# A gated delta-rule recurrence: spreading the decays with TensorE and adding the kept state in PSUM

## The chip, the cores and the metric

The kernel runs on one core of a Trainium2 chip. The metric is the time of one execution on the device, in microseconds (us). The kernel before takes 7533.77 us, the median of 3 runs (7531.89 to 7543.39).

## The reference

Two layers over x of shape (16, 512, 256). Only the recurrent attention of the first layer matters here. It has 16 heads with keys, queries and values of 64, made from the normed x by a projection, a causal convolution over 4 tokens and a silu; a (the decay, one per head and value row) and beta are sigmoids of projections.

```python
def step(S, inp):
    qt, kt, vt, at, bt = inp
    err = jnp.einsum('bhij,bhj->bhi', S, kt) - vt
    S = at[..., None] * S - bt[..., None, None] * (err[..., None] * kt[:, :, None, :])
    o = jnp.einsum('bhij,bhj->bhi', S, qt)
    return (S, o)
```

The rest (norm and gate of o, output projection, a small expert layer, then a second layer of attention) runs after the recurrence and is not touched.

## The kernel before, in words

`layer0_recurrence` cuts the 512 tokens into chunks of C = 16 and the 16 batch entries into two groups of 8, which gives 64 steps; step s works on group s mod 2. Inside a chunk the recurrence is solved token by token on 128 partitions (8 batch entries x 16 heads); between chunks the state `st[g]` (128 partitions = two heads x 64 key rows, 8 batch entries, 8 head pairs, 64 value columns) is multiplied by the decay of the whole chunk and gets the chunk's outer products added.

Each engine has a list of its own, written out by hand: a function `slot(s, ...)` per engine, called once per step, the middle ones in a hardware loop of two slots per turn. Slot s works on several steps at once: the projections and the convolution of step s + 1, the norm, gates and first projections of step s + 2, the solve of step s, and the state update of step s - 1. The engines meet only in semaphores. Each engine, and each DMA queue (SP's and ACT's), runs its list strictly in order, so that the order of the list is part of the schedule.

- **PE** (L499 to L516): `project` of step s + 1, banks 2 to 5 (L480; banks 2 and 3 wait for the end of the solve of step s - 1, `eb` at L809, as they overwrite `rows_bank`); `update` banks 0 and 1; `gates` of step s + 2 (L461: two transposes, then two gate banks of four matmul instructions of L471 and two of L472 each); `update` banks 2 to 7; `betas`; `front2` (L435, keys and values transposed); `products` (L443); `project` banks 0 and 1 of step s + 2. `update` (L418) makes 8 banks of 8 small matmuls into two PSUM banks `d_bank` in turn. An f32 matmul stands in the trace as two MATMUL instructions.
- **ACT** (L654): copies of the convolution banks (`evict`, L529), `silu`, `seed_rows`, `place_keys`, `gates` (L631), the shares of tokens 0, 1 and 2 (`shares`, L591, which POOL needs), `betas`, `front2` (L567, which ends with the write of `v_dram`, L580), `products` (L607), `evict` of banks 0 and 1, the last shares.
- **DVE** (L812): the 18 tap groups of the convolution (`conv`, L698, L709) with the norm between them, then `decay` (L713, L717: one 128x4096 multiply of the whole state by `db`, both in SBUF), the 8 adds of `state` (L720, L727: d_bank + st into st), two before the solve and two after each of its rows 0, 1 and 2, and the 16 rows of `solve` (L755), ended by `eb` (L809).
- **POOL** (L355): scales the values (L375), makes the running products of the decays (L377, L379), of which the last, `acb` (L383), is the decay of the chunk, and then accumulates the outputs row by row (L392 to L401); it waits for ACT's shares of rows 0, 1 and 2.
- **SP's queue** (L269 to L340), in this order: load x; write `upd_dram` (waits for the solve of step s - 1); load `kp`; scatter `xd` in 8 DMAs; load `qp`; load `db` (two DMAs of 1024 KB each, each decay row broadcast to 64 partitions, L313); wait for the write of `v_dram` and load `vb`, `ab`, `nb` of step s + 1 (L321 to L327); write `decay_dram` of step s (L334); write the outputs of step s - 1 (L340).

`db` and `prod` are one buffer, `decay_or_prod`. Most records of the waits of SP's queue stand at L102, a helper that only counts a semaphore up.

## Time and profile before

| | |
|---|---|
| median of 3 runs | 7533.77 us |
| the profiled execution | 7556.31 us |
| its span | 7554.5 us |
| busy PE / DVE / ACT / POOL | 5300.0 / 5952.4 / 4118.6 / 4525.3 us |
| mean granted clock of TensorE | 0.769 of full speed |

The recurrence takes about the first 4600 us of the span; the rest is the end of layer 0 and layer 1. In the timeline a row gives the start, the busy time, the engine, the line and the operation, with a count where equal instructions follow one another; what stands in square brackets is idle time before it and what ended it. The granted clock is 1.00 at 2.4 GHz and 0.50 at 1.2 GHz.

### The profile page before, as it was taken

To read this page: it belongs to the slowest core of one execution; us is meant where nothing else is said; L and a number is where in the kernel's file an instruction comes from. 1 tells how busy PE (TensorE), PEld (TensorE's weight loads), DVE (VectorE), ACT (ScalarE), POOL (GpSimd) and SP (SyncE) were. 2 spreads that over 40 slices of the span, in tenths; PEclk is the share of its full clock that TensorE was granted. 3 is DMA by queue.
4 is the path that set the end of the run, shared out by engine and by line. 5 is a ranking of instruction groups with operands and counts; after the bars stand their busy time and mean duration, and the time that the engine had idled before them with its cause. 6 is when DMAs were issued, how large, how long until landed. Compare 5 with 4: busy or idle time off the path is not lost. (4 is left out here: it accounts for less than half of the span.)

```text
span 7554.5 us, 144722 instructions
## 1 busy us (share of the span) xinstructions
PE 5300.0 (70%) x42311; PEld 3469.5 (46%) x42311; DVE 5952.4 (79%) x15810; ACT 4118.6 (55%) x10434; POOL 4525.3 (60%) x3976
## 2 busy tenths in 40 slices
PE   5666667666666666666666643777777777787777
PEld 4455555455555555555554532334333334333343
DVE  6999999999999999999999984555656566665665
ACT  5666666666666666666666642444444444444444
POOL 4999999999999999999999992111111111111110
PEclk7767777777777777777777766888888888888888
DMA  3545555555555455455455431111111111111111
GB/s 99 135 116 118 133 125 116 129 132 116 119 135 121 115 135 126 115 126 134 114 118 135 118 93 46 48 47 46 46 47 44 42 42 42 44 44 42 42 42 35
DMA packets 953133, 684.14 MB, mean 91 GB/s; under 512 B 836660, under 2 KB 888532, under 8 KB 938197
## 3 DMA queue, kind: packets, MB, share of 16 engines
q1 hardware_dynamic: 653524, 516.82, 28.6%
q10 hardware_dynamic: 299008, 159.92, 8.9%
q8 instruction: 303, 4.96, 0.3%
q14 instruction: 298, 2.43, 0.1%
HBM read 423.47 MB, written 253.17 MB: 90 GB/s over the span
## 5 line engine op out<-in xcount | busy, mean ns | idle before, releaser
L392 POOL TENSOR_TENSOR qp<-qp,ab 128x1024 f32<-128x1024 f32 (+15 forms) x1024 | 1434.2, 1401 | 80.4
L1145 POOL TENSOR_TENSOR ot<-ot,ln_w 128x1024 f32<-128x1024 f32 x64 | 150.5, 2352 | 1414.2 <-ACT ot L1420 1414.2
L430 PE MATMUL d_bank<-xd,kt 32*64 32x128 f32 x7936 | 779.4, 373 | 300.7 <-DVE st L727 295.8
L1564 DVE TENSOR_REDUCE nmax<-w_bank 128x1 f32<-128x512 f32 x1024 | 638.0, 684 | 333.4 <-PE w_bank L1190 325.4
L709 DVE SCALAR_TENSOR_TENSOR p_bank<-y,conv_w,p_bank 128x128 f32<-128x128 f32 x3072 | 833.4, 348 | 66.8 <-ACT p_bank L540 39.4
L430 PEld LDWEIGHTS d_bank<-xd,kt 32*64 32x64 f32 x7936 | 691.1, 193 | 416.3 <-DVE st L727 403.5
L401 POOL TENSOR_TENSOR qp<-qp,pt 128x832 f32<-128x832 f32 (+7 forms) x512 | 763.5, 1491 | 40.1
L495 PE MATMUL rows_bank<-xnT,wqkv 128*128 128x128 f32 x2048 | 370.6, 365 | 570.1 <-DVE eb L809 570.1
L495 PE MATMUL p_bank<-xnT,wqkv 128*128 128x128 f32 x4096 | 575.8, 305 | 223.2 <-ACT st L553 183.1
L802 DVE TENSOR_TENSOR rows_bank<-rows_bank,t 128x960 f32<-128x960 f32 (+14 forms) x960 | 671.9, 700 | 32.9
L495 PEld LDWEIGHTS p_bank<-xnT,wqkv 128*128 128x128 f32 x4096 | 546.9, 217 | 252.5 <-issue 252.5
L798 DVE TENSOR_TENSOR rows_bank<-rows_bank,ab 128x960 f32<-128x960 f32 (+14 forms) x960 | 661.8, 689 | 0.0
L799 DVE TENSOR_TENSOR t<-rows_bank,vb 128x960 f32<-128x960 f32 (+14 forms) x960 | 653.8, 681 | 0.0
L1150 POOL TENSOR_TENSOR x1b<-x,bias 128x256 f32<-128x256 f32 x64 | 46.3, 724 | 1012.1 <-DVE bst L1660 1012.1
L398 POOL TENSOR_TENSOR pt<-qp,vb 128x832 f32<-128x832 f32 (+7 forms) x512 | 630.6, 1232 | 0.0
L495 PEld LDWEIGHTS rows_bank<-xnT,wqkv 128*128 128x128 f32 x2048 | 360.4, 278 | 580.1 <-issue 580.1
L603 ACT ACTIVATE pt<-vb,qp 128x64 f32<-128x64 f32 x1920 | 472.2, 334 | 257.4 <-DVE vb L792 220.9
L603 ACT ACTIVATE share<-vb,qp 128x64 f32<-128x64 f32 x1920 | 490.3, 337 | 150.5 <-DVE vb L792 147.3
L1394 ACT ACTIVATE pt<-e_bank 128x1024 f32<-128x1024 f32 x512 | 507.7, 1018 | 105.7 <-PE e_bank L1220 102.8
L457 PE MATMUL p_bank<-st 64*32 64x80 f32 x16384 | 365.6, 234 | 149.3 <-issue 97.8
L1190 PE MATMUL w_bank<-ks,qs 96*128 96x512 bf16 x1024 | 405.6, 451 | 72.8 <-DVE nmax L1564 31.0
L379 POOL TENSOR_TENSOR eb<-eb,ab 128x64 f32<-128x64 f32 x896 | 400.5, 447 | 70.4
(203 smaller groups left out, 11701.0 us busy)
## 6 DMA issues: line engine op xcount, KB each, us to landing
decay_or_prod<-decay_dram SPq DMA_DIRECT2D x124, 1024.0 KB, 13.6
prod_dram<-decay_or_prod ACTq DMA_DIRECT2D x64, 1280.0 KB, 10.8
kp<-prod_dram SPq DMA_DIRECT2D x64, 640.0 KB, 6.6
qp<-prod_dram SPq DMA_DIRECT2D x64, 640.0 KB, 6.8
a_dram<-at ACTq DMA_DIRECT2D x64, 512.0 KB
v_dram<-vt ACTq DMA_DIRECT2D x64, 512.0 KB
vb<-v_dram SPq DMA_DIRECT2D x64, 512.0 KB, 4.0
ab<-a_dram SPq DMA_DIRECT2D x64, 512.0 KB, 8.6
```

What stands on the lines that cost most here:

```text
L392: link(nc.gpsimd.tensor_tensor(q, q, ab[:, g, r:r + 1, :].to_broadcast([128, w, DV]), ALU.mult), 0 if shared else 1)
L398: link(nc.gpsimd.tensor_tensor(pt2[:, 0:w], qp[:, g, r:C, DV + r:DV + r + 1].to_broadcast([128, w, DV]), vb[:, g, r:r + 1, :].to_broadcast ...
L401: link(nc.gpsimd.tensor_tensor(q, q, pt2[:, 0:w], ALU.add))
L430: mm = nc.tensor.matmul(d_bank[u % 2][64 * par:64 * par + 64, 128 * k:128 * k + 128], kt[32 * q:32 * q + 32, g, DK * h:DK * h + DK], xd[32 ...
L495: mm = nc.tensor.matmul(bank[:, 128 * i:128 * i + 128], wqkv[:, k, 128 * m:128 * m + 128], xnT[:, g, k, :], start=k == 0, stop=k == 1)
L603: last = nc.scalar.activation(shares_of(r)[:, t - r], vb[:, g, r, :], ACT.Copy, scale=qp[:, g, t, DV + r:DV + r + 1])
L709: nc.vector.scalar_tensor_tensor(out=zz, in0=y[:, m, :, tap:tap + C], scalar=conv_w[:, m, tap:tap + 1], in1=zz, op0=ALU.mult, op1=ALU.add) ...
L798: link(nc.vector.tensor_tensor(rows, rows, ab[:, g, r:r + 1, :].to_broadcast([128, w, DV]), ALU.mult), 1)
L799: link(nc.vector.tensor_tensor(t2[:, 0:w], column.to_broadcast([128, w, DV]), vb[:, g, r:r + 1, :].to_broadcast([128, w, DV]), ALU.mult))
L802: link(nc.vector.tensor_tensor(rows, rows, t2[:, 0:w], ALU.add))
L1394: nc.scalar.activation(pt[:, kt % 2, 2 * pr:2 * pr + 2], e_bank[pr][:], ACT.Exp, scale=float(D1) ** -0.5).then_inc(e_freed, 1)
L1564: nc.vector.tensor_reduce(nmax[:, n:n + 1], bank[:], AX.X, ALU.max, negate=True).then_inc(freed, 1)
```

## The change

The 128x4096 multiply goes. Instead, the decays of a step are loaded in their compact form into `decays` (8 partitions: one per pair of batch entries and head parity; 32 KB in two DMAs), and a matmul with a 0/1 matrix `spread` writes them over the 128 partitions of a `d_bank`. DVE multiplies the kept state by that bank (128x512, eight times a slot). TensorE then writes the kept state into the same bank with an identity matmul and adds the chunk's outer products there (`start=False`), and ScalarE copies the bank into `st`. The eight banks go in four pairs; the matmuls of a pair alternate between its two banks, which read different 32-row parts of `kt`.

```diff
+DECAY_AFTER_BANK, DECAY_AFTER_ROW = {1: 0, 4: 1}, {0: 2, 2: 3}
+def state_part(u):
+    return 2 * (u // 4) + u % 2, u // 2 % 2
...
-    decay_dram = [dram(f"decay_dram{g}", [2, GB * HP, DV]) for g in range(GROUPS)]
+    decay_dram = [dram(f"decay_dram{g}", [GB * H, DV]) for g in range(GROUPS)]
...
-        decay_or_prod = sb("decay_or_prod", [128, GB * HP * DV])
+        prod = sb("prod", [128, GB, 4 * ROW])
+        decays = sb("decays", [8, 2, HP, DV])
+        spread = sb("spread", [8, 4, 128])
...
                 if updates(lo - 1, hi - 1):
                     t = s - 1
+                    sp.wait_ge(*dma_of(dec_wr, n, g, -1))
+                    held(sp, sp_passed)
+                    if due(8 * t):
+                        sp.wait_ge(spread_done, 8 * t)
+                        held(sp, sp_passed)
+                    for par in range(2):
+                        rows = decay_dram[o].rearrange("(q b m two) i -> two q b m i", two=2, b=2, m=HP)[par]
+                        sp.dma_start(decays[4 * par:4 * par + 4], rows).then_inc(db_in[o], 16)
                     sp.wait_ge(solve_chain, SOLVE_OPS * (t + 1))
...
-                    sp.wait_ge(*dma_of(dec_wr, n, g, -1))
-                    held(sp, sp_passed)
-                    for par in range(2):
-                        rows = decay_dram[o][par:par + 1].to_broadcast([64, GB * HP, DV])
-                        sp.dma_start(db[64 * par:64 * par + 64], rows).then_inc(db_in[o], 16)
...
+            def spread_decays(s, n, g, p):
+                if p == 0:
+                    pe.wait_ge(*dma_of(db_in, n, g, 0, 32))
+                if due(8 * s + 2 * p):
+                    pe.wait_ge(d_freed, 8 * s + 2 * p)
+                held(pe, pe_passed)
+                for e in range(2):
+                    q, hh = state_part(2 * p + e)
+                    nc.tensor.matmul(d_bank[e][:], spread[:, q, :],
+                                     decays[:, :, 4 * hh:4 * hh + 4, :].rearrange("r b h i -> r h b i"),
+                                     start=True, stop=True).then_inc(spread_done, 1)
+            def update(s, n, g, p):
+                if p == 0:
                     pe.wait_ge(f_freed, front2_use(s) + 2)
                     pe.wait_ge(*dma_of(xd_in, n, g, 0, 16 * GB))
+                pe.wait_ge(decayed, 8 * s + 2 * p + 2)
+                held(pe, pe_passed)
+                for e in range(2):
+                    q, hh = state_part(2 * p + e)
+                    kept = st[g][:, 2 * q:2 * q + 2, 4 * hh:4 * hh + 4, 0:DV].rearrange("p b h i -> p h b i")
+                    nc.tensor.matmul(d_bank[e][:], ident[:], kept, start=True, stop=False)
+                last = [None, None]
+                for k in range(4):
+                    for par in range(2):
+                        for e in range(2):
+                            q, hh = state_part(2 * p + e)
                             h = 2 * (4 * hh + k) + par
+                            last[e] = nc.tensor.matmul(d_bank[e][64 * par:64 * par + 64, 128 * k:128 * k + 128],
+                                                       kt[32 * q:32 * q + 32, g, DK * h:DK * h + DK],
+                                                       xd[32 * q:32 * q + 32, h, :, :], start=False, stop=k == 3)
+                for mm in last:
                     mm.then_inc(d_filled, 1)
...
+                if state:
+                    spread_decays(*before, 0)
+                if front:
                     for j in range(2, CONV_BANKS):
                         project(s + 1, 1 - g, j)
+                if state:
+                    update(*before, 0)
+                    spread_decays(*before, 1)
+                if ahead:
+                    transposed(s + 2, g)
+                    gate(s + 2, g, 0)
+                if state:
+                    update(*before, 1)
+                    spread_decays(*before, 2)
+                if ahead:
+                    gate(s + 2, g, 1)
+                if state:
+                    update(*before, 2)
+                    spread_decays(*before, 3)
+                if ahead:
                     betas(s + 2, g)
+                if state:
+                    update(*before, 3)
+                if front:
                     front2(s + 1, n + g, 1 - g)
                     products(s + 1, n + g, 1 - g)
...
+            def keep_state(s, g, p):
+                for u in range(2 * p, 2 * p + 2):
+                    act.wait_ge(d_filled, 8 * s + u + 1)
+                    q, hh = state_part(u)
+                    nc.scalar.activation(st[g][:, 2 * q:2 * q + 2, 4 * hh:4 * hh + 4, 0:DV],
+                                         d_bank[u % 2][:].rearrange("p (h b i) -> p b h i", h=4, b=2), ACT.Copy).then_inc(d_freed, 1)
...
+            def decay(s, g, p):
                 dve.wait_ge(p_filled, 8 * (s + 1))
+                for u in range(2 * p, 2 * p + 2):
+                    dve.wait_ge(spread_done, 8 * s + u + 1)
+                    q, hh = state_part(u)
+                    kept = st[g][:, 2 * q:2 * q + 2, 4 * hh:4 * hh + 4, 0:DV]
+                    nc.vector.tensor_tensor(kept, d_bank[u % 2][:].rearrange("p (h b i) -> p b h i", h=4, b=2), kept,
+                                            ALU.mult).then_inc(decayed, 1)
```

On ACT the slot's order becomes: evict and silu of banks 2 to 5 as before, `keep_state` 0, the copy of the transposed x, silu of bank 4, `seed_rows`, `keep_state` 1, silu of bank 5, `place_keys`, `gate` 0, `keep_state` 2, `gate` 1 (with the write of `a_dram`), shares of tokens 0 and 1, `keep_state` 3, the share of token 2, `betas`, `front2`, `products` and the rest as before. On DVE `decay` 0 stands behind the last tap of convolution bank 1, `decay` 1 behind that of bank 4, `decay` 2 behind row 0 of the solve and `decay` 3 behind row 2; the eight adds are gone. Eight small copies at the start make `spread` from the identity.

## Rows read from the trace of the kernel before

**Rows 1.** Waits of 1000 to 4000 us: us in total, times, longest
```profile
PE rows_bank L495 <- DVE eb L809: 400.1, 43, 12.2
...
DVE st L717 <- DMA decay_or_prod<-decay_dram: 97.6, 43, 4.1
...
POOL vb L375 <- POOL qp L395: 24.6, 43, 0.9
```

**Rows 2.** Windows of 1000 us: span, then busy us of PE, PEld, DVE, ACT, POOL, clock, DMA
```profile
1000.00:2000.00 1000.00, 684.87 (x7278) 525.59 (x7280) 937.45 (x2259) 634.79 (x1775) 925.53 (x840) 0.73 0.53 123
```

**Rows 3.** Timeline of POOL, 2124 to 2134 us
```profile
2124.25 4.43 POOL L377 COPY eb<-ab 128x64 f32<-128x64 f32 x1
2128.76 5.48 POOL L379 TENSOR_TENSOR eb<-eb,ab 128x64 f32<-128x64 f32 x14
```

**Rows 4.** Timeline of DVE at the same time
```profile
2123.89 4.70 DVE L717 TENSOR_TENSOR st<-st,decay_or_prod 128x4096 f32<-128x4096 f32 x1 [1.81 <-DMA decay_or_prod<-decay_dram]
```

**Rows 5.** Lines by form, 1000 to 4000 us: count, busy us, mean ns, idle before
```profile
L430 PE MATMUL d_bank<-xd,kt 32*64 32x128 f32 x5472 | 541.3, 375 | 192.3 <-DVE st L727 189.7 <-DMA xd<-upd_dram 2.4
...
L471 PE MATMUL f_bank<-wa,xnT 128*128 128x512 f32 x344 | 279.9, 961 | 23.6 <-ACT xnT L629 23.6
...
L457 PE MATMUL p_bank<-st 64*32 64x80 f32 x11008 | 242.7, 232 | 109.3 <-issue 72.6 <-ACT decay_or_prod L612 30.6
L727 DVE TENSOR_TENSOR st<-d_bank,st 128x512 f32<-128x512 f32 x344 | 221.7, 686 | 21.8
...
L472 PE MATMUL f_bank<-ba,ones 1*128 1x512 f32 x172 | 130.2, 844 | 0.0
...
L575 ACT ACTIVATE kt<-f_bank 128x512 f32<-128x512 f32 x86 | 51.4, 598 | 25.7 <-PE f_bank L440 22.6
```

**Rows 6.** Timeline of PE in two slots
```profile
2053.85 1.98 PE L471 MATMUL f_bank<-wa,xnT 128*128 128x512 f32 x4
...
2101.23 6.66 PE L495 MATMUL rows_bank<-xnT,wqkv 128*128 128x128 f32 x32 [11.19 <-DVE eb L809]
...
2113.97 1.96 PE L430 MATMUL d_bank<-xd,kt 32*64 32x128 f32 x32
2118.00 0.69 PE L465 MATMUL f_bank<-ident,xn 128*128 128x128 f32 x2 [2.06 <-DVE xn L753]
2119.23 3.78 PE L471 MATMUL f_bank<-wa,xnT 128*128 128x512 f32 x4 [0.55 <-ACT xnT L629]
2122.94 2.07 PE L472 MATMUL f_bank<-ba,ones 1*128 1x512 f32 x2
...
2130.66 3.68 PE L430 MATMUL d_bank<-xd,kt 32*64 32x128 f32 x32
```

**Rows 7.** Windows: ten us in which PE never stops
```profile
2124.00:2134.00 10.00, 10.00 (x40) 4.95 (x38) 9.71 (x9) 3.93 (x11) 8.90 (x16) 0.50 0.08 13
```

**Rows 8.** Timeline of ACT: a first share, betas, and the issue of v
```profile
2061.48 3.93 ACT L603 ACTIVATE pt<-vb,qp 128x64 f32<-128x64 f32 x16 [3.96 <-DVE vb L792]
...
2074.98 0.36 ACT L646 ACTIVATE bt<-f_bank,bb 16x128 f32<-16x128 f32 x1 [0.26 <-PE f_bank L477]
...
2079.63 0.59 ACTq L580 DMA_DIRECT2D v_dram<-vt  x1
```

**Rows 9.** Timeline of SP: issues in order
```profile
2086.00 0.39 SPq L321 DMA_DIRECT2D vb<-v_dram  x1
...
2094.27 0.57 SPq L334 DMA_DIRECT2D decay_dram<-acb  x1
...
2104.46 4.10 SPq L300 DMA_DIRECT2D xd<-upd_dram  x8
```

**Rows 10.** DMA issues, 1000 to 4000 us: KB each, median us from issue to landing
```profile
xd<-upd_dram SPq DMA_DIRECT2D x344, 64.0 KB, 3.2
...
decay_dram<-acb SPq DMA_DIRECT2D x43, 32.0 KB, 6.3
beta_dram<-bt ACTq DMA_DIRECT2D x43, 8.0 KB, 1.4
```

More of the change, by code:

```diff
@@ L333, in slot @@
                         held(sp, sp_passed)
-                    sp.dma_start(decay_dram[g].rearrange("two m i -> m two i"), acb[:]).then_inc(dec_wr[g], 16)
+                    sp.dma_start(decay_dram[g], acb[:]).then_inc(dec_wr[g], 16)
                 if valid(lo - 1, hi - 1):
@@ L459, in products, with transposed @@
                     mm.then_inc(p_filled, 1)
[L461 removed]
+            def transposed(s, g):
                 bank = use(front1_use(s), 0)
@@ L467, in gates, with gate @@
                 pe.wait_ge(f_freed, front1_use(s) + 1)
-                for j in range(2):
-                    bank = use(front1_use(s), 1 + j)
-                    for k in range(2):
-                        nc.tensor.matmul(bank[:], xnT[:, g, k, :], wa[:, k, 512 * j:512 * j + 512], start=k == 0, stop=False)
-                    nc.tensor.matmul(bank[:], ones[:], ba[:, 512 * j:512 * j + 512], start=False, stop=True).then_inc(f_filled, 1)
+            def gate(s, g, j):
+                bank = use(front1_use(s), 1 + j)
+                for k in range(2):
+                    nc.tensor.matmul(bank[:], xnT[:, g, k, :], wa[:, k, 512 * j:512 * j + 512], start=k == 0, stop=False)
+                nc.tensor.matmul(bank[:], ones[:], ba[:, 512 * j:512 * j + 512], start=False, stop=True).then_inc(f_filled, 1)
             def betas(s, g):
@@ L629, in transposed, with gate @@
                 nc.scalar.activation(xnT[:, g].rearrange("p k t -> p (k t)"), bank[:, 0:2 * P], ACT.Copy).then_inc(f_freed, 1)
[L631 to L632 removed]
+            def gate(s, n, g, j):
+                if j == 0 and due(dma_of(a_wr, n, g, -1)[1]):
                     act.wait_ge(*dma_of(a_wr, n, g, -1))
[L634 to L640 removed]
+                bank = filled(front1_use(s), 1 + j)
+                nc.scalar.activation(at[:, 512 * j:512 * j + 512], bank[:], ACT.Sigmoid).then_inc(f_freed, 1)
+                if j == 1:
+                    act.wait_ge(f_freed, front1_use(s) + 3)
+                    if due(dma_of(ab_in, n, g, -2)[1]):
+                        act.wait_ge(*dma_of(ab_in, n, g, -2))
+                    act.dma_start(a_dram[g].rearrange("t b h i -> b t (h i)"), at[:]).then_inc(a_wr[g], 16)
+            def keep_state(s, g, p):
[4 more added lines that the diff above has]
+                                         d_bank[u % 2][:].rearrange("p (h b i) -> p b h i", h=4, b=2), ACT.Copy).then_inc(d_freed, 1)
             def betas(s, n, g):
@@ L654, in slot @@
             def slot(s, n, g, lo, hi):
-                if valid(lo + 1, hi + 1):
+                front, ahead, state = valid(lo + 1, hi + 1), valid(lo + 2, hi + 2), updates(lo - 1, hi - 1)
+                if front:
                     for j in range(2, CONV_BANKS):
@@ L692, in _ @@
             nc.vector.memset(ones[:], 1.0)
+            dve.wait_ge(ident_done, 2)
+            for q in range(4):
+                for par in range(2):
+                    r = 4 * par + q
+                    nc.vector.tensor_copy(spread[:, q, 64 * par:64 * par + 64], ident[0:8, r:r + 1].to_broadcast([8, 64]))
             nc.vector.memset(halo[:], 0.0).then_inc(init_done, 1)
@@ L802, in solve @@
                         link(nc.vector.tensor_tensor(rows, rows, t2[:, 0:w], ALU.add))
-                    for u in range(adds, min(adds + ADDS_PER_ROW, 8)):
-                        if update:
-                            state(s - 1, 1 - g, u)
-                        adds += 1
+                    if update and r in DECAY_AFTER_ROW:
+                        decay(s - 1, 1 - g, DECAY_AFTER_ROW[r])
                 dve.wait_ge(pool_chain, POOL_OPS * s + DECAY_OPS + 1)
@@ L823, in more_taps @@
                         conv(s + 1, k)
+                        j, tap = k // (TAPS - 1), k % (TAPS - 1)
+                        if update and tap == TAPS - 2 and j in DECAY_AFTER_BANK:
+                            decay(s - 1, 1 - g, DECAY_AFTER_BANK[j])
                 if valid(lo + 2, hi + 2):
@@ L828, in slot @@
                     more_taps()
-                if update:
-                    decay(s - 1, n - 1 + g, 1 - g)
-                if update:
-                    for u in range(ADDS_BEFORE):
-                        state(s - 1, 1 - g, u)
                 if valid(lo, hi):
```

88 lines of the change are left out of this document (27 added, 61 removed).

## The prediction

> **What bounds the kernel now.** I read first the waits of the stretch 1000 to 4000 us [rows 1]. Each wait stands there 43 times, so that a slot takes 3000 / 43 = 69.8 us. DVE waits for one thing alone, the broadcast decays (97.6 / 43 = 2.3 us a slot); POOL for nothing but its own last instruction (0.6 us); PE is idle 9.3 us a slot until `eb` lets it overwrite `rows_bank`. The window of 1000 us [rows 2] gives busy times: DVE 94%, POOL 93%, PE 68%, ACT 63%, at a granted clock of 0.73. So DVE and POOL have no room, and PE has some. The timeline then shows that the two are tied: while DVE multiplies the whole state [rows 4], a POOL copy of 64 elements takes 4.43 us [rows 3], ending where DVE's multiply ends. The 14 products of the same 64 elements behind it take 5.48 / 14 = 0.39 each. The multiply thus costs POOL some 4.0 us as well.
>
> **What goes.** On DVE the multiply of 4.7 and the wait of 2.3 go; eight multiplies replace eight adds of the same shape with the same operand in PSUM, at 0.69 each [rows 5]. DVE's own work falls to 69.8 - 7.0 = 62.8 us a slot. POOL, with the stall of 4.0 gone, falls to 65.8. Were that all, POOL would bound there. Eight copies of 8x64 at the start cost under 3 us once, which I leave out. 127 MB of broadcast writes go too; no other stage waits for those.
>
> **What comes, a price each.** An f32 matmul is two MATMUL instructions.
> - Spread: two matmuls of 512 columns with few rows. The nearest row is L472 (one row, 512 columns): 130.2 / 86 = 1.51 us each, 3.0 a pair [rows 5]; 4.1 at the half clock, half of it, some 2.2 with its start, at full clock [rows 6].
> - Kept state by identity: as L471, 279.9 / 172 = 1.63 each, 3.3 a pair [rows 5]; 3.8 and 2.0 at the two clocks [rows 6].
> - The outer products of a pair: 541.3 / 43 / 4 = 3.1 as they are [rows 5]. Now they alternate between row parts too, as L457 does, which takes 22 ns for 80 columns against 99 ns for 128, 2.8 times less per column [rows 5]. Bounds 1.1 and 3.1; I take 1.3, near L457, whose pattern it is. An update is 3.3 + 1.3 = 4.6 (3.1 to 7.5 with both clocks).
> - ACT's two copies of 128x512: 1.2 [rows 5], with handovers 1.5. DVE's two multiplies: 1.4.
> - A gate bank stays as it is, (279.9 + 130.2) / 86 = 4.8 [rows 5], 3.1 to 5.9 by the clock.
> - The landing of `decays`, 16 KB a DMA: between 1.4 (8 KB) and 6.3 (`decay_dram`, 32 KB) [rows 10]; I take 2.0, near the smaller.
>
> **Where it lies.** Before, an update needed its `d_bank` for PE and DVE alone, with two banks taking turns. Now a pair holds both banks from its spread to the end of ACT's copies, so nothing of one pair overlaps the next: spread, multiply, identity, products, copies, four times. And both ends of this chain hang on other lists. Spread 0 stands at the head of PE's slot, ahead of `project` 2, and waits for the compact decays. Those are loaded by SP behind the landing of `decay_dram`, which SP writes only after `vb`, `ab` and `nb`, which wait for `v_dram`, which ACT issues after `front2`; and `front2` now comes behind update 3 on PE, and behind `keep_state` 3 and share 2 on ACT. That closes a ring. From the start of spread 0:
> 1. Spread 0: 3.0.
> 2. `project` 2 to update 0, with ACT's copies and silus between, as in the timeline, 2101.23 to 2113.97 [rows 6]: 12.7, sum 15.7.
> 3. Update 0 and its copies, 4.6 + 1.5: 21.8.
> 4. Spread 1, 3.0, sum 24.8; the transposes up to the gate, 2118.00 to 2119.23, 1.2 [rows 6]; gate 0, 4.8 (covers multiply 1); update 1 and copies, 6.1: 36.9.
> 5. Spread 2, 3.0; gate 1, 4.8 (covers multiply 2); update 2 and copies, 6.1: 50.8.
> 6. Spread 3, 3.0; multiply 3, 1.4 (covers `betas`); update 3 and copies, 6.1: 61.3. ACT's gate copy (1.3 with its DMA issue) and shares 0 and 1 (3.9 and 3.7, from 3.93 for 16 [rows 8]) end at 59.7, just hidden.
> 7. Share 2, 3.5, then `betas` and `front2` to the issue of v, 4.7 [rows 8]: 69.5.
> 8. Until SP issues `vb`, 2079.63 to 2086.00, 6.4 [rows 8, 9]; to the write of the decays, 8.3 [rows 9]; its landing, 6.3 [rows 10]: 90.5.
> 9. Second issue and landing of `decays`, 0.6 + 2.0: 93.1, and spread 0 of the next slot.
>
> That is 23.3 us more than 69.8, in each of 62 slots with an update: 1445 us. DVE is no cover: it waits inside its list for spread 0 and 1 (with the convolution taps queued behind) and for spread 2 and 3 (with the rows of the solve behind). POOL waits for share 0, which stands behind `keep_state` 2 and gate 1. On SP the wait for `decay_dram` now holds back the write of `upd_dram`, `kp`, the scatter of `xd` and `qp`. The scatter takes 4.1 to issue and 3.2 to land [rows 9, 10], about 3 after the `upd_dram` issue; with 15.7 us from spread 0 to update 0 this stays covered, by some 5 us, and would cost directly if the projections got faster. Sum: 7556 (profiled execution) + 1445 = 9001; the median of the runs stands 23 below that execution, so 8980.
>
> **The clock, where row and rule differ.** In the trace PE is busy for all of ten us, and the granted clock stays at 0.50 [rows 7], with gate and update matmuls of the very kinds that the change adds. It is 1.00 for some of them in other slots [rows 6]. The mean prices above hold that mixture.
> The Trainium skill (TensorE: Matmul & The Clock Gate, "What's actually happening") says the array is throttled by default and that sustained activity releases it. By that rule a PE that the change fills would be granted full clock, and the sum would be rival 1's; these rows speak against it.
>
> **Rivals.**
> 1. Full clock throughout, 15%. PE is busier, so the gate opens. Spreads 4 x 0.8, updates 4 x 1.5, gates 2 x 1.7 and 0.6 of the landing less: 93.1 - 13.2 = 79.9, so 7556 + 62 x 10.1 = 8182, less 23: 8160. For: the full-clock rows. Against: rows 7.
> 2. The ring does not close, 6%: SP writes the decays early enough (with `v_dram` landed sooner), and PE's own list bounds. PE is busy 47.8 a slot [rows 2], plus 12.0 for spreads and 13.2 for identities, less 7.4 on products, is 65.6, and four copies of 1.5 that it must wait for give 71.6: 7645. Against it: SP's order is fixed, 8.3 + 6.3 lie between `vb` and the landing.
> 3. Faster, 6%: POOL freed of DVE's multiply is what decides, and the decays arrive before `eb`. Then the slot is POOL's 65.8: 7556 - 62 x 4.0 - 23 = 7285. It needs PE at full clock, products side by side, and a spread 0 done before `project` 2, whose wait of 9.3 us [rows 1] has room for it. It decides only if the ring is under 65.8 us; I find no set of row prices with less than 79.9.
> 4. The low clock everywhere, or products no faster than now, 11%: 1.1 more per spread, 1.3 per update and 1.1 per gate give 104.9: 9709; with products at the bounds and a landing of 6.3, 115.6.
>
> **Numbers.** 60% on the forecast, whose slot I put between 86 and 102 us (8540 to 9530), as the clock's mixture lies; 2% on no change. The range takes in most of rival 1 and the forecast: 8160 to 9530. A difference of 0.2% is about what a measurement of this kernel can tell from none; 0.92 slower, 0.02 same, 0.06 faster.
>
> **What would show it.** L717's row is gone; DVE's new multiplies take about 0.69. POOL's copy L377 never takes more than 0.4, and POOL is now idle some 20 us a slot before its first add, released by ACT's share. DVE waits four times a slot for a PE spread. PE waits at the head of its slot for a DMA, for many us, and after each update for ACT's copy. Wrong it would be if DVE kept 94% busy, if PE's wait for `decays` were under 2 us, or if the clock stood at 0.9 or more.

## The result, and the profile after

The changed kernel takes 8708.95 us, the median of 4 runs (8659.45 to 8740.41), beside 7535.09 us for the kernel before on the same chip: a ratio of 1.155, with an interval of 1.1525 to 1.157. The forecast was 8980, with a range of 8160 to 9530.

| | before | after |
|---|---|---|
| the profiled execution | 7556.31 us | 8659.45 us |
| its span | 7554.5 us | 8657.6 us |
| busy PE / DVE / ACT / POOL | 5300.0 / 5952.4 / 4118.6 / 4525.3 us | 6323.4 / 5703.7 / 4321.4 / 4260.9 us |
| mean granted clock of TensorE | 0.769 | 0.765 |
| slots in the 3000 us read | 43 | 34 |

A slot takes 3000 / 34 = 88.2 us in place of 69.8. The 18.4 us more, 62 times, are 1141 of the 1174 us lost, so nearly all of the loss lies in the recurrence.

The busy times in the window from 1000 to 2000 us, with the columns of [rows 2], show that no engine is full any more: the one that works most, PE, does so for 72%.

```profile
1000.00:2000.00 1000.00, 720.54 (x6358) 427.33 (x6358) 709.07 (x1826) 549.78 (x1523) 706.63 (x667) 0.74 0.32 79
2000.00:3000.00 1000.00, 733.79 (x6117) 422.23 (x6118) 703.91 (x1796) 537.54 (x1478) 678.81 (x666) 0.72 0.29 73
```

The waits of 1000 to 4000 us (columns as in [rows 1]) say who holds whom. The two waits of before for `eb` and for the broadcast decays are not among them. PE now stands at spread 0 (L433) until the compact decays land, 341.4 / 34 = 10.0 us a slot; DVE waits 12.7 a slot for spreads and 5.5 for the load of x, which was not foreseen; POOL, which had no time to wait before, waits 22.6 a slot for ACT's first share.

```profile
POOL qp L401 <- ACT pt L643: 768.0, 34, 28.3
...
DVE st L786 <- PE d_bank L433: 432.1, 201, 7.3
...
PE d_bank L433 <- DMA decays<-decay_dram: 341.4, 34, 12.4
...
DVE norm_work L800 <- DMA xt<-in_L_attn_x: 187.7, 34, 7.2
...
PE d_bank L433 <- ACT st L687: 143.9, 102, 2.1
```

The lines by form (count, busy us, mean ns, idle before) give the prices of the new work. In a slot the spreads take 407.9 / 34 = 12.0 us, the identities 11.3, the products 4.7 (12.6 before, [rows 5]), the two gate banks (249.8 + 116.0) / 34 = 10.8, DVE's multiplies 5.4 and ACT's copies 4.4.

```profile
L433 PE MATMUL d_bank<-decays,spread 8*128 8x512 f32 x544 | 407.9, 888 | 485.3 <-DMA decays<-decay_dram 341.4 <-ACT st L687 143.9
L447 PE MATMUL d_bank<-st,ident 128*128 128x512 f32 x544 | 385.7, 849 | 0.0
...
L497 PE MATMUL f_bank<-wa,xnT 128*128 128x512 f32 x272 | 249.8, 1074 | 18.7 <-ACT xnT L669 18.7
...
L786 DVE TENSOR_TENSOR st<-d_bank,st 128x512 f32<-128x512 f32 x272 | 184.8, 688 | 432.2 <-PE d_bank L433 432.1
...
L454 PE MATMUL d_bank<-xd,kt 32*64 32x128 f32 x4352 | 159.7, 286 | 0.0
...
L687 ACT ACTIVATE st<-d_bank 128x512 f32<-128x512 f32 x272 | 148.1, 601 | 578.6 <-PE d_bank L454 577.7
...
L498 PE MATMUL f_bank<-ba,ones 1*128 1x512 f32 x136 | 116.0, 945 | 0.0
```

The timelines of one slot show the ring. PE first: it waits at spread 0, runs through the four pairs with short waits for ACT's copies, and waits again at the next spread 0.

```profile
2071.64 3.75 PE L433 MATMUL d_bank<-decays,spread 8*128 8x512 f32 x4 [11.61 <-DMA decays<-decay_dram]
...
2088.00 1.88 PE L447 MATMUL d_bank<-st,ident 128*128 128x512 f32 x4
2089.81 1.10 PE L454 MATMUL d_bank<-xd,kt 32*64 32x128 f32 x32
2092.46 2.01 PE L433 MATMUL d_bank<-decays,spread 8*128 8x512 f32 x4 [1.54 <-ACT st L687]
...
2110.17 3.78 PE L497 MATMUL f_bank<-wa,xnT 128*128 128x512 f32 x4
...
2115.88 3.78 PE L447 MATMUL d_bank<-st,ident 128*128 128x512 f32 x4
2119.59 1.98 PE L454 MATMUL d_bank<-xd,kt 32*64 32x128 f32 x32
2122.86 3.75 PE L433 MATMUL d_bank<-decays,spread 8*128 8x512 f32 x4 [1.28 <-ACT st L687]
...
2163.57 2.04 PE L433 MATMUL d_bank<-decays,spread 8*128 8x512 f32 x2 [12.08 <-DMA decays<-decay_dram]
```

ACT, from the copies of pair 3: two rows later than those of pair 2 comes share 0, and the issue of v comes last.

```profile
2121.63 1.08 ACT L687 ACTIVATE st<-d_bank 128x512 f32<-128x512 f32 x2 [11.25 <-PE d_bank L454]
...
2124.07 3.92 ACT L643 ACTIVATE pt<-vb,qp 128x64 f32<-128x64 f32 x16 [0.86 <-ACT at L675]
...
2132.62 1.09 ACT L687 ACTIVATE st<-d_bank 128x512 f32<-128x512 f32 x2 [1.06 <-PE d_bank L454]
2133.59 3.44 ACT L643 ACTIVATE pt<-vb,qp 128x64 f32<-128x64 f32 x14
...
2141.49 0.59 ACTq L620 DMA_DIRECT2D v_dram<-vt  x1
```

SP's queue: `vb`, `ab`, `nb`, then the decays are written and, behind the write of the outputs (`o_dram`) and the load of x, loaded.

```profile
2147.92 0.39 SPq L327 DMA_DIRECT2D vb<-v_dram  x1
...
2157.19 0.33 SPq L340 DMA_DIRECT2D decay_dram<-acb  x1
...
2158.99 0.74 SPq L272 DMA_DIRECT2D xt<-in_L_attn_x  x1
2160.09 1.32 SPq L290 DMA_DIRECT2D decays<-decay_dram  x2
```

The view of the line that writes the decays shows that the write lands in 3.3 us on the median, not in the 6.3 of [rows 10], and in 1.9 to 6.4. The waits of SP's queue show that the load of the decays waited for this landing in 14 of the 34 slots only, for 8.7 us in all.

```profile
DMA to landing us min/median/max: 1.9/3.3/6.4
```

```profile
SPq L107 <- DMA decay_dram<-acb: 8.7, 14, 1.6
```

Last, POOL's copy beside DVE's work. The view of one line gives its shortest, median and longest duration in ns, first of the kernel before, then of the one after: the copy of 64 elements that took 4.43 us beside the SBUF multiply [rows 3] is never longer than 0.302.

```profile
L377 POOL COPY eb<-ab x43: 235/4432/4506, 1006.5 to 3939.6; 128x64 f32<-128x64 f32 x43
```

```profile
L383 POOL COPY eb<-ab x34: 233/238/302, 1051.3 to 3953.9; 128x64 f32<-128x64 f32 x34
```

### The profile page after: what moved, and what is told of

It is laid out like the page before. It is cut to its first block and busy times, and to the rows that moved or that the text cites. A ratio compares the mean times of both kernels' runs of the same rounds, so it can differ in the third digit from the quotient of the medians.

```text
span 8657.6 us, 150075 instructions
## 1 busy us (share of the span) xinstructions
PE 6323.4 (73%) x44295; PEld 3489.6 (40%) x44295; DVE 5703.7 (66%) x15756; ACT 4321.4 (50%) x10930; POOL 4260.9 (49%) x3976
## 5 line engine op out<-in xcount | busy, mean ns | idle before, releaser
L398 POOL TENSOR_TENSOR qp<-qp,ab 128x1024 f32<-128x1024 f32 (+15 forms) x1024 | 1416.6, 1383 | 80.4
L433 PE MATMUL d_bank<-decays,spread 8*128 8x512 f32 x992 | 742.5, 886 | 893.2 <-DMA decays<-decay_dram 630.2
L401 POOL TENSOR_TENSOR qp<-qp,pt 128x1024 f32<-128x1024 f32 (+1 forms) x128 | 286.3, 2237 | 1418.1 <-ACT pt L643 1408.6
L786 DVE TENSOR_TENSOR st<-d_bank,st 128x512 f32<-128x512 f32 x496 | 337.2, 689 | 800.5 <-PE d_bank L433 799.9
L687 ACT ACTIVATE st<-d_bank 128x512 f32<-128x512 f32 x496 | 270.1, 601 | 1066.2 <-PE d_bank L454 1064.6
L447 PE MATMUL d_bank<-st,ident 128*128 128x512 f32 x992 | 707.9, 854 | 2.6 <-DVE st L786 2.6
L433 PEld LDWEIGHTS d_bank<-decays,spread 8*128 8x128 f32 x992 | 219.3, 243 | 1129.3 <-issue 1129.3
L775 DVE SCALAR_TENSOR_TENSOR rows_bank<-y,conv_w,rows_bank 128x128 f32<-128x128 f32 x1536 | 429.2, 348 | 334.6 <-ACT rows_bank L580 334.6
L497 PE MATMUL f_bank<-wa,xnT 128*128 128x512 f32 x512 | 467.4, 1068 | 35.9 <-ACT xnT L669 35.9
```

The costliest lines, as they stand in the source:

```text
L398: link(nc.gpsimd.tensor_tensor(q, q, ab[:, g, r:r + 1, :].to_broadcast([128, w, DV]), ALU.mult), 0 if shared else 1)
L433: nc.tensor.matmul(d_bank[e][:], spread[:, q, :], decays[:, :, 4 * hh:4 * hh + 4, :].rearrange("r b h i -> r h b i"), start=True, stop=Tru ...
L447: nc.tensor.matmul(d_bank[e][:], ident[:], kept, start=True, stop=False)
L775: nc.vector.scalar_tensor_tensor(out=zz, in0=y[:, m, :, tap:tap + C], scalar=conv_w[:, m, tap:tap + 1], in1=zz, op0=ALU.mult, op1=ALU.add) ...
```

## The experiments

The theory, T: the time is set by the ring of the prediction (spread 0, four pairs one after the other, `front2`, `v_dram`, SP's queue, the decays, spread 0). Its rivals: TensorE's list alone is too long now; the pairing of banks costs; something other than the decays waits on the same chain. All changes "per slot" are differences of medians divided by the 62 slots; the kernel before was measured anew beside each group of runs, on the same chip (7535 to 7542 us).

| kernel | median us | ratio to before | per slot to before |
|---|---|---|---|
| the change | 8708.95 | 1.1547 [1.1525, 1.157] | +18.9 |
| decays sent early | 8269.18 | 1.0986 [1.0961, 1.1011] | +11.8 |
| and x early | 8094.56 | 1.0741 [1.0715, 1.0768] | +9.0 |
| and shares early | 7951.04 | 1.0518 [1.0476, 1.056] | +6.7 |
| no identities | 8401.67 | 1.1153 [1.1133, 1.1172] | +13.9 |
| spread 0 later | 8389.21 | 1.1122 [1.1102, 1.1143] | +13.7 |
| before, pairs only | 7538.08 | 0.9999 [0.999, 1.0009] | 0.0 |
| before, narrow multiply | 7330.85 | 0.9732 [0.9716, 0.9748] | -3.4 |
| adds on DVE | 7635.68 | 1.0119 [1.0092, 1.0145] | +1.6 |
| half in PSUM | 7420.87 | 0.9829 [0.9803, 0.9854] | -1.9 |
| the same again | 7412.40 | 0.9828 [0.9814, 0.9841] | -2.1 |
| the same, decays late | 7503.74 | 0.9950 [0.9934, 0.9965] | -0.6 |

### The decays sent early

On SP's queue the write of `decay_dram` and the load of `decays` move ahead of `vb`, `ab` and `nb`; nothing else changes. This cuts the ring at the place where T says that it closes.

```diff
                 if valid(lo, hi):
...
+                if updates(lo, hi):
+                    sp.wait_ge(pool_chain, POOL_OPS * s + DECAY_OPS)
...
+                    sp.dma_start(decay_dram[g], acb[:]).then_inc(dec_wr[g], 16)
...
+                        sp.dma_start(decays[4 * par:4 * par + 4], rows).then_inc(db_in[g], 16)
```

> The changed kernel with one thing moved: SP writes the decays of a step and loads them back in their compact form ahead of the loads of vb, ab and nb, one slot earlier than the spread needs them. Ring theory (the slot is as long as the way from spread 0 over the updates, front2, v_dram, SP's issues, the landing of decay_dram and the load of decays back to spread 0): PE's wait of 10.0 us a slot for decays goes, and with it SP's part of the ring; the slot falls from 88.2 us to 76 to 80, so 7950 to 8200 us. Rival, the serial pairs alone (spread, multiply, update, copy, four times, with the gates between, fill the slot whatever SP does): within 2 us of 88, so 8600 to 8750 us. Second rival, PE at the half clock bounds: 85 to 88.

It measured 8269.18 us (8252.31 to 8301.08), above the expected range (7950 to 8200): 7.1 us a slot come back, not 18.9. PE's wait for the decays has gone from the waits, so that ring is open; but the following waits are left, by 1000 to 4000 us with 37 slots.

```profile
POOL qp L401 <- ACT pt L643: 570.0, 36, 21.0
...
DVE norm_work L800 <- DMA xt<-in_L_attn_x: 194.9, 37, 6.7
```

POOL still waits 570.0 / 37 = 15.4 us a slot for share 0, and DVE 5.3 for x. Two more rings run through the same chain. One is SP's: x is loaded behind `nb`, whose turn also comes after `v_dram`. The other is POOL's: share 0 on ACT, POOL's rows, the scaled values for the next solve, DVE's first rows with multiply 2 behind row 0, update 2 and `keep_state` 2 on ACT, and the next share 0.

### And x early

x is loaded one step earlier, ahead of the decays on SP.

```diff
+                if valid(lo + 3, hi + 3):
+                    sp.wait_ge(xn_ready, s + 3)
+                    held(sp, sp_passed)
+                    load_x(n + 1 + g, 1 - g)
```

> The kernel with early decays, in which SP also loads x one slot earlier, ahead of the loads of vb, ab and nb. With early decays alone DVE waited 5.3 us a slot for x and 1.7 us for POOL's scaled values, at a slot of 81 us. Theory A, two rings are left, SP's tail after v_dram (vb, ab, nb, then x, then DVE's norm) and POOL's (row 0 of the solve, multiply 2, update 2, keep_state 2, gate 1, share 0, then POOL's accumulation to the scaled values of the next slot): DVE's wait for x goes, POOL's ring stays and holds the slot at 79 to 81 us, 8130 to 8260 us. Rival, SP's tail alone is left: 75 to 77 us, 7890 to 8010 us.

It measured 8094.56 us (8089.10 to 8122.02), between the two expectations. DVE's wait for x is gone; in its place DVE waits for POOL's scaled values (166.6 / 38 = 4.4 a slot), and POOL for ACT.

```profile
POOL qp L403 <- ACT pt L645: 546.2, 38, 22.0
...
DVE rows_bank L840 <- POOL vb L383: 166.6, 34, 6.9
```

The timeline of POOL in one slot shows why: released by share 0 at 2055.54, it starts the next scaling at 2110.64, 55.1 us later and without a long wait between, and the copy behind it ends at 2112.7, where DVE starts its rows (2112.57, idle 4.07). With the 8.5 us from the last scaling (2029.51) to the wait, and the wait of 15.2 itself, POOL's turn fills the slot of 3000 / 38 = 78.9.

```profile
2055.54 2.38 POOL L403 TENSOR_TENSOR qp<-qp,pt 128x1024 f32<-128x1024 f32 x1 [15.18 <-ACT pt L645]
...
2110.64 1.90 POOL L383 TENSOR_TENSOR vb<-vb,nb 128x1024 f32<-128x1024 f32 x1 [0.87 <-POOL qp L403]
2112.48 0.24 POOL L385 COPY eb<-ab 128x64 f32<-128x64 f32 x1
```

### And the shares early

ACT's shares 0, 1 and 2 move ahead of the copies of pairs 1, 2 and 3 (`keep_state`). In the change shares 0 and 1 come behind the copy of pair 2, and share 2 behind that of pair 3.

```diff
                 if state:
                     keep_state(s - 1, 1 - g, 0)
...
+                if valid(lo, hi):
+                    shares(s, n, g, FIRST_SHARES[0:0 + 1])
                 if state:
                     keep_state(s - 1, 1 - g, 1)
```

> As the kernel with early decays and early x, but ACT's shares of token 0 and 1 stand ahead of keep_state 1 and keep_state 2, and that of token 2 ahead of keep_state 3. Theory A, this opens POOL's ring: share 0 is done 5 us after the start of the solve instead of 25, and POOL's own ring is 66 us; what is left is PE's list of some 65 busy us with its waits for ACT's copies, a slot of 75 to 77.5 us, 7890 to 8050 us. Rival, POOL's wait for share 0 was slack: no faster than early decays and early x.

It measured 7951.04 us (7893.37 to 7968.98), as expected. DVE no longer waits for POOL's values; POOL's wait for share 0 falls to 274.8 / 39 = 7.0, and DVE waits 553.6 / 39 = 14.2 for PE's spreads. With all three rings opened, 12.2 of the 18.9 us are back. POOL is still not free of ACT: it waits (274.8 + 172.0) / 39 = 11.5 a slot for its shares. By these waits, what is left of the loss, 6.7, lies with TensorE's list and its handovers with DVE and ACT; no run takes them apart.

```profile
DVE st L810 <- PE d_bank L437: 553.6, 206, 8.5
...
POOL qp L405 <- ACT pt L660: 274.8, 43, 8.2
```

### No identities

From the change, the identity matmuls are taken out, and the products start the bank. The kept state is left out of the sum, so `st` holds the new products alone.

```diff
-                    nc.tensor.matmul(d_bank[e][:], ident[:], kept, start=True, stop=False)
...
-                                                       xd[32 * q:32 * q + 32, h, :, :], start=False, stop=k == 3)
+                                                       xd[32 * q:32 * q + 32, h, :, :], start=True, stop=True)
```

> The changed kernel without the identity matmuls; the kept state is left out of the sum, so that the state is the chunk's products alone. In the changed kernel they took 385.7 us in 34 slots, 11.3 us a slot. Ring theory: all four lie in the ring, two of them at the full clock; the slot falls by 10 to 11 us to 77 to 78, so about 8010 to 8090 us. Rival, DVE or SP sets the slot by itself and PE has slack: no more than 2 us a slot, 8580 us or more.

It measured 8401.67 us (8390.17 to 8420.97), 5.0 us a slot and not the 11.3 that the identities take: well above the 8010 to 8090 expected, and below the rival's 8580. The lines by form say where the rest went. The spreads, untouched, take 526.7 / 36 = 14.6 us a slot for 12.0, the products 5.8 for 4.7, and the wait for ACT's copies 214.5 / 36 = 6.0 for 4.2: 5.5 of the 11.3 given back, which leaves 5.8. The mean granted clock is 0.736, below the 0.765 of the change.

```profile
L433 PE MATMUL d_bank<-decays,spread 8*128 8x512 f32 x574 | 526.7, 1068 | 586.1 <-DMA decays<-decay_dram 371.7 <-ACT st L683 214.5
...
L450 PE MATMUL d_bank<-xd,kt 32*64 32x128 f32 x4608 | 208.1, 332 | 0.0
```

So the clock is no constant of the program: with less work in the same chain of waits, TensorE was granted less, and the spreads and the products became dearer by 3.7 us a slot. Not every matmul did: the gate matmuls kept their price (1067 ns for 1074), and those of one row took 783 for 945. The window of 1000 to 2000 us has PE busy for 670 us at 0.69, against 721 at 0.74 in the change.

### Spread 0 later

In the change, spread 0 moves behind `project` 2 and 3 on PE, and multiply 0 behind bank 2's taps on DVE. If PE's wait at spread 0 holds the projections back for nothing, part of it is covered.

```diff
-DECAY_AFTER_BANK, DECAY_AFTER_ROW = {1: 0, 4: 1}, {0: 2, 2: 3}
+DECAY_AFTER_BANK, DECAY_AFTER_ROW = {2: 0, 4: 1}, {0: 2, 2: 3}
...
+                    for j in range(2, 4):
+                        project(s + 1, 1 - g, j)
                 if state:
                     spread_decays(*before, 0)
-                    for j in range(2, CONV_BANKS):
+                    for j in range(4, CONV_BANKS):
```

> The changed kernel with spread 0 moved behind project 3 on PE, and multiply 0 behind bank 2 of the convolution on DVE. PE's wait for the decays then no longer holds back project 2 and 3, which can start at eb. Ring theory: the ring gets shorter by the projections 2 and 3 (5 to 6 us at that point) and by part of what ACT and DVE do behind them; the slot falls from 88.2 us to 82 to 84.5, 8320 to 8480 us. Rival, the ring runs over SP's late write of upd_dram and xd alone, which the move leaves where it is: within 1 us of 88.2, 8640 us or more.

It measured 8389.21 us (8377.52 to 8413.39), as expected: 5.2 us a slot. PE's wait for the decays is 191.7 / 36 = 5.3 where it was 10.0. The waits for x and for share 0 stay. The two projection banks are covered by the ring, as its steps say. The clock again does not stay where it was: with every matmul of the change kept, PE is busy for 791 of the 1000 us, more than the 721 of the change, at 0.69 instead of 0.74.

### Before, with the banks in pairs

The pairing alone: the kernel before with the products of two banks alternating, and no other change. It asks whether the pairing costs or brings anything by itself.

```diff
-                for u in banks:
-                    q, hh = u // 2, u % 2
...
+                for p in range(banks[0] // 2, banks[-1] // 2 + 1):
...
+                            for e in range(2):
+                                q, hh = state_part(2 * p + e)
```

> The kernel before with its eight update banks in pairs as in the change, adds on DVE as before. PE's matmuls of an update go from 12.6 us a slot to about 4.6 (1.1 per pair measured in the changed kernel); PE waited 9.3 us a slot for eb and is on no ring. Ring theory: within 0.5% of 7535 us. Rival, PE's updates hold up the shares or front2 and so POOL: faster by 1 to 4 us a slot, 7290 to 7470 us.

It measured 7538.08 us (7531.90 to 7554.30, 10 runs) at a ratio of 0.9999 [0.999, 1.0009]. The products take 292.1 / 43 = 6.8 us a slot instead of 12.6, and PE waits longer in return: 352.6 / 43 = 8.2 a slot for DVE's adds where it was 4.4 [rows 5], and as long as before for `eb`. PE was no bound before, and so its gain is worth nothing there. The run changes two things at once, the turn between two banks and the turn between row parts; which of them makes the products cheaper it can't say.

```profile
L437 PE MATMUL d_bank<-xd,kt 32*64 32x128 f32 x5472 | 292.1, 376 | 353.8 <-DVE st L735 352.6 <-DMA xd<-upd_dram 1.2
```

### Before, with a narrow multiply

The kernel before, with DVE's multiply cut to 1 of 64 value columns. The decay of the other 63 is left out. This prices what the change takes away from DVE and POOL.

```diff
-                sv = st[g][:, :, :, 0:DV]
+                sv = st[g][:, :, :, 0:1]
```

> The kernel before with DVE's multiply narrowed to one of the 64 value columns; the decay is left out for the other 63. The broadcast load and all waits stay. Theory that POOL bounds the kernel before and is stalled by the wide multiply: POOL's slot falls from 69.8 to 65.8 us and DVE, whose load of decays takes the same time, falls from 69.8 to about 66; the time falls by 62 x 4.0 us, to about 7290 us. Rival, the way of DVE's eb over upd_dram, xd and the broadcast load bounds alone: DVE gains its 4.3 us, the same time, but POOL's copy at L377 still takes 4.4 us in most slots. Rival, POOL is not stalled by it: POOL stays at 69.8 us and the time within 0.5% of 7535.

It measured 7330.85 us (7321.40 to 7345.10): 3.4 us a slot, somewhat less than the 4.0 expected (7290). The multiply falls from 4.7 to 0.76, and POOL's copy with it: the longest takes 312 ns. DVE and POOL are still the fullest, 921 and 912 of 1000 us, and DVE still waits 93.4 / 45 = 2.1 for the broadcast. So 3.4 us a slot are won by the freed DVE and POOL alone; what removing the wait for the broadcast would add no run shows.

```profile
L717 DVE TENSOR_TENSOR st<-st,decay_or_prod 128x64 f32<-128x64 f32 x45 | 34.4, 764 | 93.4 <-DMA decay_or_prod<-decay_dram 93.4
```

### The adds on DVE

With decays and x early, TensorE spreads the decays as in the change, but the kept state goes another way: DVE multiplies from PSUM and also adds the products, as before. The identities and ACT's copies are gone. The shares are early too, and on ACT gate 0 stands behind share 1.

```diff
+KEPT_IN_PSUM = (False, False, False, False)
+AFTER_TAP = {5: [('d', 0)], 11: [('a', 0)], 15: [('d', 1)]}
+AFTER_ROW = {0: [('a', 1)], 2: [('d', 2)], 3: [('a', 2)], 5: [('d', 3)], 6: [('a', 3)]}
...
+                    nc.vector.tensor_tensor(kept, d_bank[u % 2][:].rearrange("p (h b i) -> p b h i", h=4, b=2), kept,
+                                            ALU.add).then_inc(d_freed, 1)
```

> Spread by TensorE and the multiply from PSUM kept, but the identity matmuls and ACT's copies taken out again: DVE adds the update as in the kernel before, eight multiplies and eight adds a slot. Decays and x early, pairs placed wider apart. DVE's own work is 63.3 us a slot in the changed kernel plus 8 x 0.69 of adds less what they overlap, 68.5; POOL is free of the stall at 65.8, PE is at 55. Theory A: the slot is DVE's, 68.5 to 69.5 us, 7440 to 7520 us, at or just under the kernel before. Rival, the serial use of the two banks holds DVE in waits of 3 us and more a slot: over 7600 us.

It measured 7635.68 us (7610.65 to 7649.21), a miss: expected was a gain over the kernel before. DVE is busy for 925 of 1000 us, at a granted clock of 0.71. PE waits for DVE's adds (L820), and the adds for PE's products: each pair goes PE, DVE, PE, DVE before its banks are free, inside two lists that have other work between. DVE itself waits 95.0 / 42 = 2.3 us a slot for the products, about 2 more for ACT's copies of convolution banks, and never for a spread. The time lies where the rival of the expectation put it (over 7600 us, DVE held by the serial use of the two banks), though that wait is less than its 3 us and more; no run tests it.

```profile
PE d_bank L437 <- DVE st L820: 241.3, 126, 4.2
...
DVE st L820 <- PE d_bank L460: 95.0, 90, 2.8
```

### Half in PSUM, half on DVE

Between the two: pairs 0 and 3 keep their state in PSUM and are copied by ACT, pairs 1 and 2 are added by DVE. Decays and x are loaded early, ACT makes shares 0, 1 and 2 after the copy of pair 0 and before that of pair 3, spread 0 stands behind `project` 3, and multiplies and adds have new places in DVE's list.

```diff
+KEPT_IN_PSUM = (True, False, False, True)
+AFTER_TAP = {8: [('d', 0)], 15: [('d', 1)], 17: [('a', 1)]}
+AFTER_ROW = {1: [('d', 2)], 2: [('a', 2)], 3: [('d', 3)]}
```

> Pairs 0 and 3 keep their state in PSUM (identity matmul, ACT's copy), pairs 1 and 2 are added by DVE. DVE sheds four adds, 65.8 us of its own, POOL is at 65.8, PE gains 6.6 us to some 61. Theory A: a slot of 67 to 68.5 us, 7340 to 7450 us, under the kernel before by 1 to 2.5%. Rival, PE at the half clock cannot serve four chains in a slot: 70 us or more, 7550 us or more.

It measured 7420.87 us (7394.35 to 7433.27). The same kernel once more:

> The hybrid once more with more rounds, on the same chip as the two others, for its interval: 7390 to 7440 us, a ratio of 0.981 to 0.986 to the kernel before.

7412.40 us (7398.91 to 7430.36), a ratio of 0.9828 [0.9814, 0.9841]. It is faster than both kernels. Its slot is 3000 / 44 = 68.2 us where [rows 1] give 69.8, and the window with the columns of [rows 2] has all engines fuller than in the change.

```profile
1000.00:2000.00 1000.00, 803.88 (x7942) 495.31 (x7942) 931.12 (x2374) 661.65 (x1857) 886.40 (x846) 0.77 0.40 99
```

POOL's wait for share 0 is down to 120.1 / 44 = 2.7 us a slot, and DVE's for spreads to 1.2.

The same kernel with the write and load of the decays put back where the change has them:

```diff
+                    for par in range(2):
+                        rows = decay_dram[o].rearrange("(q b m two) i -> two q b m i", two=2, b=2, m=HP)[par]
...
-                    sp.dma_start(decay_dram[g], acb[:]).then_inc(dec_wr[g], 16)
...
-                    for par in range(2):
-                        rows = decay_dram[g].rearrange("(q b m two) i -> two q b m i", two=2, b=2, m=HP)[par]
...
+                    sp.dma_start(decay_dram[g], acb[:]).then_inc(dec_wr[g], 16)
```

> The hybrid with one thing undone: SP writes the decays behind nb and loads them at the head of the next slot, as in the change. With front2 no longer held back by share 0 and 1, v_dram is issued some 33 us after the solve starts, so the ring is shorter than DVE's list by little or not at all. Ring theory: slot of 69.5 to 71.5 us, 7500 to 7630 us, slower than the hybrid by 1 to 3%. Rival, SP's place for the decays matters only with the long ring: within 0.5% of the hybrid, 7390 to 7460 us.

7503.74 us (7494.19 to 7509.73): 1.3 to 1.5 us a slot dearer, and PE waits 107.0 / 43 = 2.5 for the decays again. The same fault that accounts for 7.1 us in the change accounts for 1.4 here; by T that is because the rest of the ring is shorter, as PE's wait says (2.5 for 10.0).

```profile
PE d_bank L436 <- DMA decays<-decay_dram: 107.0, 38, 4.6
```

## Why the prediction was right, and what it missed

**The steps of the ring.** Measured from one spread 0 to the next (us from its start), in two slots, of which the timelines above show the second, and on the mean of the 34 slots that start between 1000 and 4000 us, against the prediction's sums:

| | predicted | slot at 1985.72 | slot at 2071.64 | mean of 34 |
|---|---|---|---|---|
| update 0 starts | 15.7 | 16.4 | 16.4 | 16.5 |
| spread 1 | 21.8 | 20.8 | 20.8 | 21.1 |
| gate 0 | 26.0 | 23.7 | 24.0 | 24.8 |
| spread 2 | 36.9 | 32.4 | 35.5 | 35.0 |
| spread 3 | 50.8 | 46.5 | 51.2 | 48.4 |
| copies of pair 3 end | 61.3 | 56.3 | 62.1 | 58.4 |
| share 2 ends | 64.8 | 59.7 | 65.4 | 61.8 |
| v is issued | 69.5 | 64.2 | 69.9 | 66.3 |
| `vb` is issued | 75.9 | 70.6 | 76.3 | 72.7 |
| decays written (issue) | 84.2 | 79.6 | 85.6 | 80.3 |
| `decays` loaded (issue) | 90.5 | 82.1 | 88.5 | 84.6 |
| next spread 0 | 93.1 | 85.9 | 91.9 | 88.0 |

The chain ran in the predicted order and closed where predicted, in each of the 34 slots (82.0 to 94.5 us long). By the count of slots in 3000 us the mean is 88.2 where 93.1 was forecast, 4.9 less, 62 x 4.9 = 304 us, which with 8980 gives 8676 beside 8709 measured.

**What goes.** The multiply went, and so did POOL's stall (302 ns at most). The narrow multiply bears out the size: 3.4 us a slot when nothing else changes, where the prediction had room for 4.0 by POOL's bound.

**The prices.** Spread pair 3.0 as taken. Identity pair 11.3 / 4 = 2.8 for 3.3. Products of a pair 4.7 / 4 = 1.2 for 1.3; in the timeline 1.10 where the clock is high and 1.98 where it is low, so the nearest-row choice L457 was the right end. Update 4.0 for 4.6. Copies and handovers 1.28 to 1.54 of PE's wait behind the last product, for 1.5. Gate bank 5.4 for 4.8.

**The mis-sized terms.** The mean of the 34 slots is 5.1 us shorter than forecast. The largest term is SP's stretch from `vb` to the load of the decays. The prediction put it at 8.3 + 6.3 = 14.6; it takes 11.9, and lies between 11.3 and 12.5 in every slot. Step 8 counted the landing of the decays' write, 6.3 as in the kernel before, behind the issues. That is not what fills the time: the load waited for the landing in 14 slots, for 8.7 / 34 = 0.3 us a slot. The 4.3 us from the write to the load are mostly SP's own issues of `o_dram` and x, which stood in no step. The issue of x holds the queue for 0.7 to 5.6 us, and does so for longest where those of `ab` and `nb` were short. In the slot of 2071.64 `ab` and `nb` took 3.3 and 5.2 and x 0.7; in the one that starts at 1283.2 it was 1.4, 1.9 and 5.5, as the timeline of SP's queue shows:

```profile
1365.33 5.53 SPq L272 DMA_DIRECT2D xt<-in_L_attn_x  x1
1371.13 1.29 SPq L290 DMA_DIRECT2D decays<-decay_dram  x2
```

Update 0 with its copies took 4.6 for 6.1 (1.88 and 1.10 for its matmuls in the slot above, at a granted clock of 1.00), and the way from gate 0 to spread 2 10.2 for 10.9. The other stretches from spread 1 to the issue of v were each shorter by 0.5 us or less. On the other side update 0 started 0.8 later, and from the load's issue to spread 0 it was 3.4 for 2.6.

**What would show it.** L717 is gone; DVE's multiply takes 0.69; POOL waits 22.6 a slot (some 20 foreseen); PE waits at the head of its slot for a DMA, and 143.9 / 102 = 1.4 us behind an update for ACT's copy. Not quite right: DVE was to wait four times a slot for a spread. Of its eight multiplies 201 / 34 = 5.9 waited, but the two at spread 0 mostly had their delay already behind them, in the wait for x.

**What was missed.** "That closes a ring" was true and "DVE is no cover" too, but the prediction spoke as if there were one ring. There are three on the same chain, close in length: with the decays early, 7.1 us a slot come back; x and share 0 then hold the next 2.8 and 2.3. What SP issues behind `nb`, the load of x and the write of `o_dram`, stood in no step; the POOL wait for share 0 was named and not followed round to the values that the next solve needs. The cover of the `xd` scatter held, as predicted (some 5 us): PE never waits for it in the change, and does so by 51.5 / 38 = 1.4 us a slot when decays and x are early.

**The rivals.** Rival 1, full clock, 8160: against it the measured clock of 0.74 and 0.72 in two windows, with PE 72% and 73% busy. The first window below has PE busy for all of 11.3 us, in gate 1 and update 2, at a granted clock of 0.50, as in [rows 7]. The other two lie just before it: 0.50 with PE busy throughout, then 0.99 with PE idle for almost half of the time.

```profile
2110.20:2121.50 11.30, 11.30 (x43) 4.40 (x42) 7.27 (x10) 0.17 (x1) 0.00 (x0) 0.50 0.01 1
2101.40:2104.40 3.00, 3.00 (x5) 1.12 (x4) 0.54 (x1) 0.00 (x0) 1.00 (x1) 0.50 0.00 0
2104.40:2107.10 2.70, 1.50 (x33) 0.86 (x32) 0.00 (x0) 1.15 (x3) 0.00 (x0) 0.99 0.00 0
```

The Trainium skill (TensorE: Matmul & The Clock Gate, "What's actually happening") holds that sustained activity releases the throttle; the trace of the change does not bear that out in these stretches. The run without identities went the way of that sentence, though: less work, less clock (0.69 with PE 67% busy). The run with spread 0 later did not: 0.69 with PE 79% busy. Why the clock falls where it does stays open; the run without identities alone took one kind of matmul away, and it changed the waits as well. Rival 2 (a ring that does not close) is refuted by PE's wait of 10.0. Rival 3 (faster by POOL's freedom) failed, since the ring is above 65.8; its prize is real, as the narrow multiply and the half-PSUM kernel show. Rival 4 (dear products, low clock everywhere): the products took 1.2 a pair.

**Open.** The half-PSUM kernel differs from the change in the places of several items at once, so its gain isn't split between fewer identities (half), shares and new places; only the decays' place was undone alone. It differs from the kernel with the adds on DVE in such places too (spread 0, gate 0, multiplies and adds), so that step isn't split either.

## What to carry to other kernels

When work moves between engines that each run a list in order, follow each new wait round until it comes back to its start, through DMA queues too, and do so for everything that stands behind it in those lists, not only for the tensor that moved: here three rings of similar length ran through one chain, and opening one gave back 7.1 of 18.9 us a slot. Price a stretch of an in-order DMA queue by all the issues that stand in it, and not by the landing of one transfer: here a landing taken from the profile of before was counted 6.3 us and cost a wait of 0.3. And where a change frees one engine by filling another, a share of the work may be the best amount: in the orders tried here, the whole update kept in PSUM cost 5.2% with the rings open, none of it 1.2%, and half of it gained 1.7%.

## What the runs showed of the hardware

**A POOL copy held by DVE's operands.** 128x64 elements took 4.43 us beside DVE's 128x4096 multiply with both operands in SBUF [rows 3, 4], and 0.24 beside multiplies with one operand in PSUM (at most 0.302), and 0.29 with the SBUF multiply cut to 64 elements (at most 0.312). The Trainium skill (GPSIMD Engine Reference, the table of specifications) has POOL share its SBUF interfaces with VectorE, with contention for DVE instructions with two SBUF inputs; the trace agrees, and shows how much: the copy doesn't run slower throughout but ends with the multiply. Where the copy was through before the multiply began, one of the products behind it (L379, 0.32 on the median) took up to 4.59 in its place.

**Products alternating between row parts.** 32 MATMUL instructions of one pair take 1.10 us at the high clock and 1.98 at the low one. As many took 1.96 and 3.68 in the kernel before [rows 6], at granted clocks of 1.00 and 0.50. On the mean it was 3.1 a pair, and 1.7 with the alternation there (292.1 / 43 / 4).

**A clock that moves with an edit.** Taking 11.3 us of matmuls out of a slot lowered the mean granted clock from 0.765 to 0.736 and made the untouched spreads 20% dearer (1068 ns for 888) and the products 16% (332 for 286), 3.7 us of the saving, while the gate matmuls kept their price (1067 for 1074). Moving one spread, with no matmul taken out, lowered it to 0.753. The runs of one kernel differ by less: 0.757 to 0.765 in the change, 0.735 to 0.736 without identities, 0.751 to 0.753 with the spread moved.

**Small writes and the traffic around them.** The 32 KB write of the decays landed in 6.3 us on the median in the kernel before, in 3.3 (1.9 to 6.4) in the change, and in 1.4 (1.4 to 1.5) where SP issues it ahead of `vb`, `ab` and `nb`. In the change it took 1.9 at 2157.19, where `ab` and `nb` had held the queue for 8.4 us, and 4.6 at 1363.96, where they had for 3.2. The broadcast of the kernel before is not what made it long there: that was issued at 2039.20, took 13.6 us to land on the median, and was over when the write of 2094.27 [rows 9] went out.
